# Adding two relu outputs while they are transposed: plain matmuls replaced by transpose-mode matmuls in every chunk

## What is computed

```python
x = x + ssm(layernorm(x))          # in: 256 -> 2 x 512; state 16 per channel; scan over time
x = x + ffn(layernorm(x))

# ssm: h = h * exp(dt * A) + (dt * x) * B ;  y = sum over state of h * C ;  y = (y + x * D) * silu(z)
# ffn, E = 4 experts that share Wi and Wo, each with its own low-rank part, the best 2 of each row:
base = x @ Wi.T                                    # (rows, 1024)
h    = relu(base[:, None, :] + lora)               # one per expert
out  = sum over the 2 chosen experts of w_e * (h_e @ Wo.T)
```

## Time and profile before

| | |
|---|---|
| runs | 1996.81 us median of 3 (1984.02 to 1997.95) |
| the profiled execution | 1996.33 us, its span 1994.5 us |
| PE busy | 1719.9 us, 86% of the span |
| weight loads of PE | 934.9 us, 47% |
| DVE busy | 1823.7 us, 91% |
| ACT busy | 1422.9 us, 71% |
| POOL busy | 1793.7 us, 90% |
| traffic with HBM | 117 GB/s mean |

### The profile page before, as it was taken

How to read it: one execution, slowest core, us unless ns; L and a number is a source line. 1 busy time by engine, 2 the same in 40 slices (tenths; PEclk the granted TensorE clock), 3 DMA queues, 4 the chain that set the end, 5 groups by cost and what they waited for, 6 DMA issues and landing times.

```text
span 1994.5 us, 27643 instructions
## 1 busy us (share of the span) xinstructions
PE 1719.9 (86%) x7776; PEld 934.9 (47%) x7776; DVE 1823.7 (91%) x2246; ACT 1422.9 (71%) x2755; POOL 1793.7 (90%) x780
## 2 busy tenths in 40 slices
PE   3365769898998989899898989989898998988999
PEld 1112225555544545454454555445455544545565
DVE  2799999999999999999999999999999999999941
ACT  3566767778687777868777787877778787776633
POOL 1999999999999999999999999999999999999800
PEclk8676779999999999999999999999999999999999
DMA  5546462653546365454636545463654546365100
GB/s 178 137 103 150 117 148 77 154 132 97 128 110 164 80 158 126 101 126 110 164 81 160 124 102 122 110 164 88 156 121 111 117 106 164 82 153 121 37 19 14
DMA packets 146769, 235.05 MB, mean 118 GB/s; under 512 B 22064, under 2 KB 46896, under 8 KB 146096
## 3 DMA queue, kind: packets, MB, share of 16 engines
q1 hardware_dynamic: 146608, 233.18, 48.5%
HBM read 190.11 MB, written 42.99 MB: 117 GB/s over the span
## 4 chain that ended last, share of the span: by engine, by line
DVE 26%; POOL 24%; issue 21%; PE 20%; ACT 5%; DMA 1%; SPq 0%; DVEq 0%; POOLq 0%; ACTq 0%
POOL hs L1344 12%; DVE decay L1286 11%; POOL hs L1356 7%; DVE hs L1276 6%; DVE hs L1286 4%; PE bank L932 4%; PE bank L868 3%; PE y_ps L946 3%; PE bank L910 2%; POOL e_dt L1334 2%; PE bank L884 2%; PE bank L927 2%; POOL z_dt L1323 1%; ACT decay L1089 1%; ACT xin L1047 1%
## 5 line engine op out<-in xcount | busy, mean ns | idle before, releaser
L1344 POOL TENSOR_TENSOR hs<-dx_rep,b_rep 128x2048 f32<-128x2048 f32 x256 | 1161.0, 4538 | 31.4 <-PE y_ps L946 19.2
L1286 DVE TENSOR_TENSOR_SCAN decay<-decay,state,hs 128x512 f32<-128x512 f32 x640 | 797.2, 1274 | 37.8 <-ACT decay L1089 33.9
L1089 ACT ACTIVATE decay<-dt_rep,a_sb 128x512 f32<-128x512 f32 x1024 | 694.3, 686 | 29.0 <-DMA dt_rep<-rep_scratch 10.6
L1286 DVE TENSOR_TENSOR_SCAN hs<-decay,state,hs 128x512 f32<-128x512 f32 x384 | 487.6, 1270 | 4.6 <-ACT decay L1089 3.0
L1356 POOL TENSOR_TENSOR hs<-hs,c_rep 128x1024 f32<-128x1024 f32 x192 | 454.7, 2368 | 4.1 <-ACT state L1103 4.1
L1276 DVE TENSOR_TENSOR hs<-decay,c_rep 128x1024 f32<-128x1024 f32 x320 | 384.7, 1202 | 0.0
L946 PE MATMUL y_ps<-hs,nsum 128*32 128x512 f32 x2048 | 299.6, 660 | 56.7 <-DVE gated L1179 27.7
L868 PE MATMUL bank<-xn_t,w_in_sb 128*128 128x512 f32 x512 | 254.4, 627 | 12.0 <-DVE silu L1174 7.4
L910 PE MATMUL bank<-w_i_sb,x_t 128*128 128x512 f32 x492 | 247.9, 627 | 13.8 <-DVE x L1190 9.2
L1103 ACT COPY state<-decay 128x2 f32<-128x2 f32 x320 | 51.0, 159 | 287.1 <-DVE hs L1276 287.0
L927 PE MATMUL bank<-ident,r 128*128 128x128 f32 x1840 | 230.8, 279 | 21.6 <-DVE x L1190 20.4
(11 more groups left out here) (149 smaller groups left out, 1750.6 us busy)
## 6 DMA issues: line engine op xcount, KB each, us to landing
dx_rep<-rep_scratch SPq DMA_DIRECT2D x256, 256.0 KB, 4.7
dt_rep<-rep_scratch SPq DMA_DIRECT2D x256, 256.0 KB, 7.6
b_rep<-bc_scratch SPq DMA_DIRECT2D x256, 64.0 KB, 3.3
rep_scratch<-z_dt SPq DMA_DIRECT2D x64, 256.0 KB, 2.5
rep_scratch<-e_dt SPq DMA_DIRECT2D x64, 256.0 KB, 2.7
c_rep<-bc_scratch SPq DMA_DIRECT2D x256, 64.0 KB, 2.2
xin<-in_u SPq DMA_DIRECT2D x16, 512.0 KB, 4.0
xr<-in_u SPq DMA_DIRECT2D x16, 512.0 KB, 4.3
```

The costliest lines, as they stand in the source:

```text
L1089: nc.scalar.activation(decay[:, j, :], dt_rep[m % 2][:, j, :], ACT.Exp, scale=a_sb[:, J * s + j:J * s + j + 1]).then_inc(decay_ready, 1)
L1286: v.tensor_tensor_scan(hs[s % 4][:, j, :] if kept else decay[:, j, :], decay[:, j, :], hs[s % 4][:, j, :], state[:, b, n:n + 1], ALU.mult, ...
L1344: nc.gpsimd.tensor_tensor(hs[s % 4][:], dx_rep[m % 2][:], b_rep[:, k, :].unsqueeze(1).to_broadcast([P, J, T]), ALU.mult).then_inc(input_re ...
```

## The change

The T job has one form for all chunks: the eight matmuls of chunks 0 to 14, now with `is_transpose=True`, the second of each block adding in PSUM to the first. In the last chunk they replace the four transposes of the sum, and DVE's job R, its eight places in the table of turn 16 and its semaphore are gone. There PE now waits, as in the other chunks, for the bank of J to be freed, which ACT does when it has written `r2`.

```diff
@@ DVE_END (one line for a step of turn 16)
-    " | R0 post |  | R1 post, R2 post",
     " |  |  | ",
-    " | R3 post |  | K0 post",
-    " | R4 post |  | ",
-    " | R5 post |  | ",
+    " |  |  | ",
+    " |  |  | K0 post",
+    " |  |  | ",
+    " |  |  | ",
     " |  | K1 post | ",
-    " | R6 post, K2 post | R7 post | ",
+    " | K2 post |  | ",
@@ semaphores
-        sp_turn, dve_turn, last_sums = sem("sp_turn"), sem("dve_turn"), sem("last_sums")
+        sp_turn, dve_turn = sem("sp_turn"), sem("dve_turn")
@@ job_pe
                 elif letter == "T":
-                    if is_last(q):
-
-                        pe.wait_ge(last_sums, i + 1)
-                        for f in range(4):
-                            mm = pe.transpose(ps[:, f * P:(f + 1) * P], r1[i % 2][:, f * P:(f + 1) * P], ident[:])
-                    else:
-
-                        wait_read(pe, c, when, "J", [i], own=b)
-                        for f in range(4):
-                            for r in (r1, r2):
-                                mm = pe.matmul(ps[:, f * P:(f + 1) * P], r[i % 2][:, f * P:(f + 1) * P], ident[:],
-                                               start=r is r1, stop=r is r2)
+                    wait_read(pe, c, when, "J", [i], own=b)
+                    for f in range(4):
+                        for r in (r1, r2):
+                            mm = pe.matmul(ps[:, f * P:(f + 1) * P], r[i % 2][:, f * P:(f + 1) * P], ident[:],
+                                           start=r is r1, stop=r is r2, is_transpose=True)
@@ job_dve
-                elif letter == "R":
-
-                    wait_read(dve, c, when, "J", (i,))
-                    v.tensor_tensor(r1[i % 2][:], r1[i % 2][:], r2[i % 2][:], ALU.add).then_inc(last_sums, 1)
```

## The result

The changed kernel takes 1996.79 us, median of 20 runs (1994.82 to 2000.13); beside it the kernel before took 1991.55, median of 20 (1978.86 to 1998.15). The ratio over all these runs is 1.0034, 95% interval 1.0019 to 1.0049 (that of the two medians is 1.0026): about a third of a per cent slower, measurably, and well within the 1% that the forecast called no change. PE's busy time fell from 1719.9 to 1651.9 us and its mean clock over the whole span from 0.936 to 0.921.

A forecast was written before the change was run, and what follows sets the result against it. In the turns, how late PE or ACT results reach DVE's strict order bounds the kernel; after about 1900 us, PE does. 1996.3 + 11 (turns) - 4 (tail) = 2003 us, range 1974 to 2030.

The forecast's parts named there:

- T from 2.0 to 0.9 us: T in chunks 0 to 14: eight transposes take 0.88 us, so one T saves 0.9 us, bounds 0.75 and 1.1.
- Rival 3: T: adding transposes run at the pace of ordinary matmuls, or are not treated as transposes; 2006 us, chance 0.06.
- The turns gain at the projections and the decays behind them: Turns: earlier projections remove DVE's 0.69 us wait for decays and maybe 0.35 for K's product; at most 1.04 a turn.
- rival 1: Turns: the clock does not fall at new places, or its fall meets slack; 1979 us, chance 0.25.
- The clock falls ahead of I0, and J0 then holds ACT: Gap before I0 grows to 3.1 us, the clock falls, late J0 holds decays; 0.9 us a turn, 0 to 1.71.
- The clock falls ahead of H0: Gaps before H0 grow to 2.7 us, the clock falls, DVE waits at the router; 1.0 us a turn, 0 to 2.08.
- K1, the third place: A wider gap before K1 could slow its product at the low clock; taken as 0, bounds 0 and 1.5 us.
- A turn: One full turn: -1.04 + 1.0 + 0.9 = +0.86 us; thirteen turns, +11 us.
- The tail: Late part of the kernel, after 1850 us, and the last chunk: -2.6 us, at best -7.1, taken as -4.
- The last chunk's own price: Last chunk: eight T jobs go from 0.44 to 0.88 us, 3.5 more, and DVE's 0.70 sum goes; 2.8 us over.
- Rival 2: Turns: new low-clock stretches at H0 and J0 cost what turn 1 shows, 2.75 us a turn; 2028 us, chance 0.17.
- Rival 4: Turns: transposes count as idle PE for the clock, K1 hit also, 4.25 us a turn; 2048 us, chance 0.06.

The follow-up runs named there:

- run 5: Changed kernel, with three ordinary 128x512 matmuls put into T7's bank before T7 in turns 1 to 14: 1985.34 us, ratio 0.9976 to the kernel before.
- run 6: Changed kernel, with 24 transposes of 128x128 put into T7's bank before T7 in turns 1 to 14: 1985.81 us, ratio 0.9980 to the kernel before.
- run 9: Kernel before, with T in chunks 0 to 14 as four ordinary matmuls of r1 alone, r2 left out: 1994.28 us, ratio 1.0027.
- run 1: Kernel before, with transpose mode for T in chunks 0 to 14 only, the last chunk unchanged: 1993.96 us, ratio 1.0035.
- run 12: Changed kernel, J0's two base matmuls ahead of I0 and its bank wait, ACT's copy of T7 one unit forward: 1991.34 us, ratio 1.0007 to the kernel before.
- run 2: Changed kernel, with transposes of both relu outputs in the last chunk only, chunks 0 to 14 as before: 1987.70 us, ratio 0.9991 to the kernel before.

## Why the prediction was right, step by step

- **T from 2.0 to 0.9 us.** Right: 0.87 to 1.04 in the chain, 1.07 by busy time. A transpose costs half of an ordinary float32 matmul here, and adding in PSUM costs nothing: eight are twice the 0.44 us of four. Rival 3 falls. The Trainium skill, "TensorE: Matmul & The Clock Gate", section Terms, has `transpose_mode` as "4× faster for FP32"; the trace does not agree, since a T job is nowhere near a quarter of its old length.
- **The turns gain at the projections and the decays behind them.** Right in kind and larger than priced. Of the 1.04 us a turn, the decays' 10.0 us fell to 1.5, while K's 0.35 stayed in each turn (4.6 in all, after 6.4). Beyond it the wait for the projection halved, 9.1 us or 0.7 a turn: K0's product in front of it is mostly hit by a low stretch of 3.4 us now instead of nearly seven and takes 3.96 us instead of 5.13. I had kept that wait at full size in the forecast, and had its shrinking only as an extra of rival 1.
- **The clock falls ahead of I0, and J0 then holds ACT.** Right in place, chain and gap, which is 3.15 us against 3.1 forecast. The price was mis-sized: 24.1 / 13 = 1.85 us a turn, above the upper bound of 1.71 that turn 1 gave and twice the 0.9 that I took. The low stretch covers all of J0's base product (3.52 us for 1.96), not half of it. Runs 5, 6 and 9 show the cause.
- **The clock falls ahead of H0.** Wrong as a rule: one turn of thirteen, at 2.25 us instead of 1.0 in each. The idle time there is 2.03 us in three pieces and not 2.7 in two: G0 and G1 both split it, and T5 came only 0.4 us earlier, not 0.9, as the job ahead of it waited for ACT's copy of T4. But the same three pieces did make the clock fall in one turn here and in four of run 5, so what decides stays open. A turn in which H0 is hit grows by more than the bound of 2.08. K1, the third place, was not hit: DVE's wait for it stayed at 0.35.
- **A turn.** Forecast +0.86, so +11 in thirteen; measured +4.3 us in all, a third of a microsecond each on average, and nothing in a settled turn. The errors nearly cancel: H0 forecast at +1.0 and mostly absent, J0 at 0.9 instead of 1.85, the projection's -0.7 not counted. That the total came out so near is in part luck. The forecast was also made against one execution of the kernel before, 5 us above the median measured later.
- **The tail.** -4 forecast, bounds -2.6 and -7.1. From the statistics job at about 1830 on it is -2.6 - 0.7 = -3.3, within them; the stretch ahead of that job gives +1.3 back. PE's waits from 1900 on are 2.5 us in all against 2.1. The last chunk's own price was 2.0, forecast 2.8.
- **Rival 1** (no new fall of the clock) is wrong as it stands, but what it would be worth can be seen: with the gap filled the kernel is at 1985, not at the 1979 forecast, while the clock still falls at other places. **Rival 2** was right for J0, where it had 1.71 us, and wrong for H0. **Rival 4** falls: transposes fill a gap as well as matmuls do (run 6), and in most turns the stretch around G0 and G1, which holds little but transposes, keeps the upper level. The Trainium skill, "TensorE: Matmul & The Clock Gate", section Part 4: PE-mode transpose, says that full rate "doesn't engage" for the transpose mode. Run 6 does not agree for float32 transposes between other work: 24 of them, 2.78 us, kept the clock up as the matmuls of run 5 did.

## What to carry to other kernels

An engine with slack has no time to sell, but it can lose some: work taken off TensorE turns into idle time in front of whatever it next waits for, and here a gap that grew from 1.3 to 3.1 us was followed by half the clock for the products behind it. Before speeding up a part of TensorE's work, find the wait at which the saved time will pile up, and what hangs on the first product after it. To fill a gap, look at where the instruction's bank wait stands: work put behind a wait on the late engine lengthens the path instead of filling it.

## What the runs showed that was not expected

The turn has preferred lengths. In the kernel before, the changed kernel and runs 1, 9 and 12, whose waits of DVE differ by place and size, it settles at 115.9 to 116.3 us for most of the run, and then the low stretches come at the same place in each turn. They last about 3.4 or about 6.8 us there. Runs 2 and 5 have turns of 113.6 us, with low stretches of 3.4 us at places where DVE loses nothing or 0.4 us by them. Why different kernels share the length is open: a coupling between the turn and the times at which the clock changes would explain it, and no run here tests that.

From 300 to 1840 us the kernel before had 16 low stretches and the changed one 28, 86 and 144 us long in all; the sums on PE show it as L946 299.6 us before and L939 311.5 after, for the same 2048 records.
